# Two-layer expert FFN on one core: common B split on GpSimd, rank matmuls moved back in the second up stage, two pieces of wi issued by SyncE

## The reference

```python
hidden_i  = x @ wi.T
hidden_i += 2 * (x @ common_wi_a.T) @ common_wi_b.T + 2 * (x @ expert_wi_a.T) @ expert_wi_b.T
hidden_i  = relu(hidden_i)
hidden_o  = hidden_i @ wo.T
hidden_o += 2 * (hidden_i @ common_wo_a.T) @ common_wo_b.T + 2 * (hidden_i @ expert_wo_a.T) @ expert_wo_b.T
out = x + hidden_o
```

## Time and profile before

| | |
|---|---|
| median of 3 runs | 120.47 us (119.81 to 123.22) |
| the profiled execution | 120.01 us |
| its span in the trace | 118.2 us |
| PE busy | 113.1 us, 96% of the span |
| DVE, ACT, POOL busy | 60.3, 47.4, 42.0 us |

### The profile page before, as it was taken

One profiled execution on the slowest core, in us unless ns is written; L12 is line 12 of the kernel. 1 busy time (PEld: TensorE's weight loads), 2 busy tenths in 40 slices (PEclk: granted clock), 3 DMA queues, 4 the chain that ended last, 5 costly groups with the idle time before them and its releaser, 6 DMA issues.

```text
span 118.2 us, 1984 instructions
## 1 busy us (share of the span) xinstructions
PE 113.1 (96%) x730; PEld 103.7 (88%) x730; DVE 60.3 (51%) x104; ACT 47.4 (40%) x94; POOL 42.0 (36%) x60
## 2 busy tenths in 40 slices
PE   6979998989999999999999999999999999999990
PEld 6758887878889999988889999988889999999990
DVE  4486999999964421134444335134444135525121
ACT  4467589343973511323663523213343113332100
POOL 2024699989899020225573006616000020000000
DMA  3999799998980035106000015006000010111121
GB/s 97 372 358 361 222 367 370 333 310 287 246 309 7 6 64 205 44 3 222 0 6 0 0 48 176 30 20 188 33 0 0 0 38 11 44 44 44 44 94 44
DMA packets 8748, 14.93 MB, mean 126 GB/s; under 512 B 1042, under 2 KB 5138, under 8 KB 8738
## 3 DMA queue, kind: packets, MB, share of 16 engines
q1 hardware_dynamic: 8018, 13.49, 34.9%
q10 hardware_dynamic: 720, 1.31, 3.2%
HBM read 12.70 MB, written 2.10 MB: 125 GB/s over the span
## 4 chain that ended last, share of the span: by engine, by line
PE 77%; DVE 11%; DMA 5%; SPq 3%; issue 1%; ACT 1%
PE bank_o L732 36%; PE bank_h L627 24%; PE bank_o L728 5%; DMA b_raw<-in_rec_b 5%; PE bank_h L661 5%; DVE hid L475 4%; DVE common_st L475 2%; PE bank_low L678 2%; PE bank_o L751 1%; DVE xT L480 1%; DVE low_stack L475 1%; PE bank_o L627 1%; PE bank_low L627 1%; DVE b_stack L491 1%; PE bank_h L704 1%
## 5 line engine op out<-in xcount | busy, mean ns | idle before, releaser
L732 PE MATMUL bank_o<-wcat,hid 128*128 128x272 f32 x336 | 45.1, 289 | 0.0
L732 PEld LDWEIGHTS bank_o<-wcat,hid 128*128 128x128 f32 x336 | 43.4, 188 | 0.0
L627 PE MATMUL bank_h<-xT,wiT 128*128 128x512 f32 x156 | 39.8, 395 | 0.6 <-DVE wiT L562 0.6
L627 PEld LDWEIGHTS bank_h<-xT,wiT 128*128 128x128 f32 x156 | 27.7, 189 | 6.4 <-issue 1.2
L475 DVE SCALAR_TENSOR_TENSOR hid<-bank_h,hid 128x512 fp32r<-128x512 f32 x26 | 17.3, 687 | 13.4 <-ACT hid L379 13.4
L379 ACT ACTIVATE hid<-bank_h 128x512 fp32r<-128x512 f32 x26 | 14.9, 598 | 17.1 <-PE bank_h L661 16.9
L552 DVE TENSOR_TENSOR o_sb<-bank_o,x_nat 128x256 f32<-128x256 f32 x16 | 6.7, 423 | 19.5 <-PE bank_o L751 17.4
L276 POOL TENSOR_TENSOR b_stack<-b_raw,b_stack 32x1024 fp32r<-32x1024 f32 x6 | 14.4, 2406 | 3.5 <-ACT b_stack L367 3.4
L267 POOL CAST a_stack<-a_raw 128x192 fp32r<-128x192 f32 x8 | 4.5, 560 | 18.1 <-DMA a_raw<-in_rec_a 18.1
L661 PEld LDWEIGHTS bank_h<-low_stack,b_stack 128*128 128x128 f32 x52 | 8.7, 189 | 2.0 <-DVE low_stack L475 0.6
L402 ACT ACTIVATE rank_sb<-bank_o 128x64 fp32r<-128x64 f32 x14 | 3.1, 223 | 18.0 <-PE bank_o L732 18.0
(11 more groups left out here) (58 smaller groups left out, 107.5 us busy)
## 6 DMA issues: line engine op xcount, KB each, us to landing
b_raw<-in_rec_b SPq DMA_DIRECT2D x8, 512.0 KB, 5.6
x_nat<-in_x_n SPq DMA_DIRECT2D x4, 512.0 KB, 3.9
out<-o_sb SPq DMA_DIRECT2D x16, 128.0 KB, 1.7
x_raw<-in_x_t SPq DMA_DIRECT2D x6, 256.0 KB, 4.0
w_raw<-in_wo_t SPq DMA_DIRECT2D x4, 256.0 KB, 5.2
w_raw<-in_wi_t ACTq DMA_DIRECT2D x3, 256.0 KB, 4.9
a_raw<-in_rec_a SPq DMA_DIRECT2D x8, 96.0 KB, 3.8
bo_raw<-in_rec_bo SPq DMA_DIRECT2D x8, 96.0 KB, 3.6
```

Source lines behind the costliest of these rows:

```text
L627: nc.tensor.matmul(up_bank(q, m)[:, :], wiT_at(sw, k, m), xT[q % 2][sx][:, k, :], start=start, stop=False)
L732: last = nc.tensor.matmul(bank_o[g % NO][:, 0:WIN], hid[q % 2][sh][:, m, tok], wcat[sw][:, m, win], start=(m == 0 and i == 0), stop=(m == ...
```

## The change

The first three parts are about the beginning of the program, the fourth about the second up stage.

1. Piece 0 of wi becomes an input tensor of its own (`wi_0`), so each half is one stretch of memory; before, it was every other kilobyte.
2. ACT's queue issues piece 1 alone. SP issues piece 2 just ahead of the two B loads of step 0, and piece 3 behind them. The splits of piece 3 on ACT and DVE go behind those of B and of the ranks of step 0.
3. The common B half is doubled, copied and split by three GpSimd instructions ahead of the A half, and `common_b` leaves DVE.
4. PE: `wo_product` 2 and 3 behind up_main(1, 2), the rank matmuls of up 1 only from behind up_main(1, 3) on. ACT and DVE do all four wo parts ahead of the first tile of up 1.

```diff
@@ SP
-                sp.dma_start(w_raw[:, 0, k * 2 * P:(k + 1) * 2 * P], wi_t[0][:, k * 2 * P:(k + 1) * 2 * P]).then_inc(wi0_in[k], 16)
+                sp.dma_start(w_raw[:, 0, k * 2 * P:(k + 1) * 2 * P], wi_0[k]).then_inc(wi0_in[k], 16)
...
+            sp.dma_start(w_raw[:, 2, :], wi_t[1]).then_inc(wi_in[2], 16)
             load_b(0)
+            sp.dma_start(w_raw[:, 3, :], wi_t[2]).then_inc(wi_in[3], 16)
@@ GpSimd, split_common
                 pool.wait_ge(common_in, 48)
+                nc.gpsimd.tensor_scalar(common_raw[:, F:], common_raw[:, F:], ALPHA, None, ALU.mult).then_inc(common_b_twice, 1)
+                pool.wait_ge(common_b_twice, 1)
+                nc.gpsimd.tensor_copy(common_st[:, F:], common_raw[:, F:]).then_inc(common_b_hi, 1)
+                pool.wait_ge(common_b_hi, 1)
+                rows = common_st[BLK:2 * BLK, F:]
+                nc.gpsimd.tensor_tensor(rows, common_raw[BLK:2 * BLK, F:], rows.bitcast(F32), ALU.subtract).then_inc(common_b_lo, 1)
+                pool.wait_ge(common_b_lo, 1)
@@ ACT, up
                 if q == 1:
-                    wo_part_hi(0)
-                    wo_part_hi(1)
+                    for i in range(PIECES):
+                        wo_part_hi(i)
                 for m in range(MF):
                     hidden_hi(q, m)
-                    if q == 1 and m == 0:
-                        wo_part_hi(2)
-                        wo_part_hi(3)
@@ DVE, first_up
-                common_b()
```

More of the change, by code:

```diff
@@ L15, with conditional_ffn @@
 STAGES = [("up", 0), ("up", 1), ("down", 0), ("up", 2), ("down", 1), ("up", 3), ("down", 2), ("down", 3)]
-def conditional_ffn(nc, x_t, x_n, ids, wi_t, wo_t, rec_a, rec_b, rec_bo, rec_ao, common, out):
+def conditional_ffn(nc, x_t, x_n, ids, wi_0, wi_t, wo_t, rec_a, rec_b, rec_bo, rec_ao, common, out):
     P = 128
@@ L22, in conditional_ffn @@
     D = KD * P
-    PIECES = wi_t.shape[0]
+    PIECES = wo_t.shape[0]
     PIECE = wi_t.shape[2]
@@ L130, in conditional_ffn @@
         common_a_hi, common_a_lo, common_b_hi, common_b_lo = (sem(f"common_{n}") for n in ("a_hi", "a_lo", "b_hi", "b_lo"))
+        common_b_twice = sem("common_b_twice")
         last_ao_hi, last_ao_lo = sem("last_ao_hi"), sem("last_ao_lo")
@@ L349, in _ @@
             nc.scalar.copy(act_warm[:, :], zeros[:, 0:1])
-            for i in range(1, PIECES):
-                act.dma_start(w_raw[:, i, :], wi_t[i]).then_inc(wi_in[i], 16)
+            act.dma_start(w_raw[:, 1, :], wi_t[0]).then_inc(wi_in[1], 16)
             def split_x_hi(q, k):
@@ L414, in first_up @@
                     split_x_hi(0, k)
-                for i in range(1, PIECES):
-                    split_wi_hi(i)
+                split_wi_hi(1)
+                split_wi_hi(2)
                 split_b_hi(0, 0)
@@ L419, in first_up @@
                 ranks_in_hi(0)
+                split_wi_hi(3)
                 for k in range(KD):
@@ L501, in hidden_lo @@
                 lo_part(hid[q % 2][LO][:, m, :], up_bank(q, m)[:, :], None, hid[q % 2][HI][:, m, :]).then_inc(hid_lo, 1)
[L503 to L508, removed]
             def wo_part_sum(i):
@@ L566, in first_up @@
                     split_x_lo(0, k)
-                for i in range(1, PIECES):
-                    split_wi_lo(i)
+                split_wi_lo(1)
+                split_wi_lo(2)
                 split_b_lo(0, 0)
@@ L571, in first_up @@
                 ranks_in_lo(0)
+                split_wi_lo(3)
                 for k in range(KD):
                     split_x_lo(1, k)
-                common_b()
                 for m in range(MF):
@@ L580, in up @@
                 if q == 1:
-                    for part in (wo_part_sum, wo_part_lo):
-                        part(0)
-                        part(1)
+                    for i in range(0, PIECES, 2):
+                        for part in (wo_part_sum, wo_part_lo):
+                            part(i)
+                            part(i + 1)
                 for m in range(MF):
                     hidden_lo(q, m)
[L586 to L589, removed]
             def down(q):
@@ L777, in second_up @@
                 wo_product(1)
+                up_main(1, 2)
+                wo_product(2)
+                wo_product(3)
+                up_main(1, 3)
                 up_lora(1, 0)
-                for m in range(2, MF):
+                up_main(1, 4)
+                up_lora(1, 1)
+                up_lora(1, 2)
+                for m in range(5, MF):
                     up_main(1, m)
[L781 to L784, removed]
+                    up_lora(1, m - 2)
+                up_lora(1, MF - 2)
                 up_lora(1, MF - 1)
@@ L846 @@
     wi_t = given["wi"].reshape(MF // 2, 2 * P, KD, P).transpose(0, 3, 2, 1).reshape(MF // 2, P, KD * 2 * P)
+    wi_0, wi_t = wi_t[0].reshape(P, KD, 2 * P).transpose(1, 0, 2), wi_t[1:]
     wo_t = given["wo"].reshape(D, MF // 2, 2, P).transpose(1, 3, 2, 0).reshape(MF // 2, P, 2 * D)
@@ L861 @@
     common = np.concatenate([given["common_wo_a"], given["common_wo_b"].T], axis=1)
-    laid = dict(x_t=x_t, x_n=x_n, ids=ids, wi_t=wi_t, wo_t=wo_t, rec_a=rec_a, rec_b=rec_b, rec_bo=rec_bo, rec_ao=rec_ao, common=common)
+    laid = dict(x_t=x_t, x_n=x_n, ids=ids, wi_0=wi_0, wi_t=wi_t, wo_t=wo_t, rec_a=rec_a, rec_b=rec_b, rec_bo=rec_bo, rec_ao=rec_ao, common=common)
     nc = bacc.Bacc("TRN2", target_bir_lowering=False, num_devices=1)
```

## The result

| | before | after |
|---|---|---|
| median | 121.33 us (119.81 to 123.22, 4 runs) | 122.04 us (121.20 to 122.65, 4 runs) |
| the profiled execution | 120.01 us | 122.11 us |
| its span | 118.2 us | 120.3 us |

The ratio is 1.0178, 95% interval 1.0128 to 1.0227: slower by 1.8%, where 118.8 us, 1.4% less, was forecast.

The account below looks back on a forecast made before the run. The prediction took the kernel as bound by PE's matmuls (113.1 of 118.2 us busy). Its terms -0.6 (A), -0.3 (B), -0.4 (C) and +0.1 (D) gave -1.2 us, from 120.01 to 118.8 us; range 118.0 to 120.1.

Parts of the forecast that it names:

- The rest, at nothing: SP's two added issues, 0.4 us each, and later loads of pieces 2 and 3 of wi: covered, no cost.
- E: Common B on GpSimd: three added instructions of 1.9 us together (1.5 to 2.5), covered before PE asks, so cost 0.
- D: New PE wait at tile 6 of step 1 for DVE's hidden tile behind four wo parts: 0.1 us, at most 0.3.
- A: PE's first wait, for the split of wi: second half of piece 0 comes earlier, -0.6 us, ends 0 and 1.0.
- B: PE's wait for a hidden tile at the ranks of step 1 goes, as common B leaves DVE: -0.3 us.
- C: PE's wait for the rest of step 1's ranks goes, as its rank matmuls come over 3 us later: -0.4 us.
- The third: Rival: GpSimd late with common B, common A and the B split, PE waits at step 1's ranks; 123.7 us, chance 0.07.
- The second: Rival: PE's first wait stays, its gain 0, the rest as forecast; -0.6 us, 119.4 us, chance 0.20.

Follow-up runs that it names:

- e6: Against the kernel before: pieces 2 and 3 of wi issued on SP's queue, piece 0 left in its old layout; median 122.82 us, ratio 1.0194.
- e9: The new PE order, with pieces 2 and 3 of wi on ACT's queue but issued behind its token casts, piece 3 split late; 120.41 us, ratio 0.996.
- e4: Common B half on GpSimd plus the new order, with the loads of before; median 121.06 us, ratio 0.9984 against before.
- e7: The new order alone plus one unread GpSimd subtraction of 32x1024 behind its B split of step 1; 120.90 us, ratio 1.0108 against before.
- e12: The new order alone plus four unread GpSimd memsets of 128x1024 behind its B split; 120.30 us, ratio 1.0007 against before.
- e3: The new order of PE's rank matmuls and the wo parts alone, loads and common B as before; 118.75 us, ratio 0.9887 against before.
- e2: The common B half on GpSimd alone, loads and PE's order as before; median 123.72 us, ratio 1.0095 against before.
- e8: The new order alone plus two unread GpSimd memsets of 128x1024 behind its B split; 119.56 us, ratio 0.9932 against before.
- e5: The new layout, the moved loads and the new order, with common B left on DVE; median 119.91 us, ratio 0.9913 against before.
- e1: The new layout of piece 0 and the moved loads alone, common B and PE's order as before; median 122.02 us, ratio 1.0131.

## Why the prediction was wrong, point by point

- **"The rest, at nothing" failed, on the loads.** It let B of step 0 come earlier, 0.4 us for the issue against 0.7 for the bytes no longer ahead of it at the rate of the earlier trace rows, and had no term for A and B of step 1. Measured: ACT's second B cast of step 0 began at 11.83 instead of 10.78, for which PE waited 0.34 us, at the rest of the ranks of step 0, and A of step 1 was 3.4 us late. Not all of the 3.4 need be the change's: A of before, at 12.75, is near the early end of its group, and the averages (16.02 and 13.80) differ by 2.2. The count took the DMA engines to be as full as before; with two pieces asked for later they moved 313 GB/s instead of 376, and from 5.5 to 6.5 us only 164. The other four kernels that ask late have the same hole (124 to 217 GB/s in its halves). e6 and e9 show that this is the time of asking. That too few bytes are asked for just then fits it, but was not shown.
- **E failed, not by its price.** 2.13 us against 1.9. The 0.9 us of cover for the B split held only if the line "begins no earlier than before", which was read as "no later"; it began 3.2 us later and PE waited, 0.28 and 0.21 us by the releasers, 0.51 and 0.46 with what lies around them.
- **D failed by size, and it is the largest loss.** 0.1 us forecast, 0.3 its end; 1.21 measured. Its worst case gave the second pair 1.88 us; that was nearly right (1.96). The first pair took 3.23 where D had 1.88, and the sums ahead of it began 1.40 us behind the first wo_product (23.73 to 25.13) where D had 0.4. The prediction had the rule in its hand, from the 2.57 us of the earlier trace rows, and asked it only about the token split. By its own times DVE's first wo split would begin at 22.6 + 0.4 + 1.38 = 24.4 and GpSimd's B split end at 25.4: already a collision of a microsecond. The rule ("SBUF — State Buffer" of the Trainium skill, section "Who interferes with whom") is that a DVE instruction with two SBUF inputs contends with a GpSimd one that reads SBUF, and not with one that only writes. The runs agree in both halves: the split that meets GpSimd's subtraction ends 0.55 us behind it (after, e4, e7), and memsets do nothing to it (e12, 1.30 the pair).
- **The wo_products 2 and 3** had no term of their own. They use the banks of 0 and 1 again, DVE's sums began at 25.13, and 0.65 us was lost. The sums were late by a path that the prediction did not price: on DVE they stand behind the hidden tiles of step 0 and the ranks of step 1, those waited for ACT's hidden tiles, and ACT had a B cast ahead of these that waited for the load of B of step 1:

```profile
18.40 1.05 ACT L377 CAST b_stack<-b_raw 128x1024 fp32r<-128x1024 f32 x1 [1.26 <-DMA b_raw<-in_rec_b]
```

```profile
19.98 1.29 DVE L483 SCALAR_TENSOR_TENSOR hid<-bank_h,hid 128x512 fp32r<-128x512 f32 x2 [1.64 <-ACT hid L389]
```

In e3 ACT's cast began at 16.16 without a wait, and the sums 0.44 us behind the first wo_product (23.11 to 23.55), as D had it.

- **A was not borne out.** The cast of the second half did begin at 5.53 (5.6 forecast), but the change need not be the reason. With the loads of before it begins anywhere from 5.14 to 6.24 in the nine profiles (5.69 on average), with the late loads from 5.16 to 5.85 (5.55). The 0.6 us was read off one execution at the late end of that spread. (The prediction's "second from 5 to 6 us" is a microsecond.) The first half came later in the changed kernel (PE's first matmuls at 4.70 instead of 4.33), and the ranks of step 0 began at 10.70 instead of 10.95: 0.25 us, not 0.6. Over all profiles they begin at 10.58 on average with the early loads and at 10.62 with the late ones, so no gain is shown. In e3, with the cast at 6.21, no wait is listed and the ranks began at 11.05. PE's first matmuls start 0.43 us apart there (4.80, 5.23, 5.65) and 0.23 before (4.68, 4.91, 5.15), and so they fill the time.
- **B and C: both waits have gone, but B's was partly one of the execution.** With common B off DVE (after, e2, e4) the ranks of step 1 do not wait; DVE reaches the hidden tiles at 17.05 instead of 18.95. But the wait is absent from e3 too, which leaves common B on DVE: its subtraction took 1.19 us there instead of 2.57 and ended at 17.08, 0.19 us after GpSimd's subtraction had begun, as A had come 0.73 us later. In e8, where A came as early as before (12.68), it took 2.58 and PE waited 0.3 again. C is part 4's: in e3 the down stage begins at 34.28, 1.10 before 35.38, of which 0.43 is there at the start of the second up stage and 0.67 is won in it, against 0.4 forecast. Around its wait of 0.41 the stretch of before lost 0.66 in all; that of e3 (13.91 us) loses nothing.
- **The rivals.** The third (GpSimd late) was right in its side and named its place, but gave the price of three slow instructions as the cause. They weren't slow; what they stood behind was late, and what they stood in front of met DVE. The second's 0 for A is nearer to the profiles than the 0.6, but whether its rule on the queues is the reason no run here shows: the half comes early and late with the same loads.

Put together: in the changed kernel two delays add up, about 3 us from the loads and 2.1 from common B, and move GpSimd's B split from the earlier trace rows 18.71 to 23.55 onto 23.75 to 28.49, beside the wo splits that the order has put there. Either alone is partly borne by the new order (e5 0.9913, e4 0.9984), the order without them wins 1.1 to 1.2%. The changed layout alone was not tried.

## What to carry to other kernels

Where work is moved to GpSimd, lay its whole later line, not just the moved instructions, against DVE's two-input instructions: a collision costs DVE the rest of GpSimd's instruction (up to 2.88 us here for 0.7), and what stands behind it on DVE pays. An early load that nobody needs yet may keep the DMA engines full; asking for it later can make everything behind it later as well. A wait in one profile can be that execution's alone, above all at a start that is fed by loads: read it in several before it is priced. When cover of one edit is counted, count it from the new start of the line and not from the old one.

## What the runs showed of the hardware that was not expected

A GpSimd instruction that nobody waits for cost the kernel about 2% (e7 against e3). A named wait of 0.64 us can be absent from another profile without any gain (A, e3). And behind a wait PE can go slower for a while. In e6 PE stands 2.45 us until 26.23; two rows of its timeline, and then two stretches behind the wait with the columns as above:

```profile
26.23 0.76 PE L664 MATMUL bank_h<-low_stack,b_stack 128*128 128x256 f32 x2 [2.45 <-POOL b_stack L278]
26.79 2.76 PE L630 MATMUL bank_h<-xT,wiT 128*128 128x512 f32 x6
```

```profile
26.80:29.30 2.50, 2.50 (x7) 1.98 (x7) 1.24 (x2) 0.60 (x1) 2.20 (x5) 0.50 0.76 248
30.00:35.00 5.00, 5.00 (x28) 4.23 (x27) 4.83 (x7) 3.64 (x6) 4.49 (x9) 1.00 0.62 176
```

The granted clock is 0.50, the lower level of 1.2 GHz, and the six matmuls of a tile take 2.76 us to their modelled end instead of 1.55. In e2 such a stretch follows the wait of 3.8 us (0.50 from 29 to 30 us); in e1 none follows that of 2.26, where the clock stays at 1.00. What decides is not shown: all four executions of e6 and four of the six of e2 have a lowered mean clock, and the changed kernel's four have none, but 6 of the 31 executions of before that stand beside e9 to e12 have one too, and the profile of before has no wait over 0.64 us. A part of e6's 1.9% may be this clock.
